# 16 bit number tables in SBUF for VectorE's one-hots, and TensorE weights read with a step, in a two-layer graph network on one Trainium2 core

## The chip, the cores and the metric

One core of one Trainium2 chip runs the whole program. The metric is device time in microseconds (us) from the first to the last instruction and what lies around it. Each engine works through its own queue of instructions and they meet by semaphores. TensorE (PE) multiplies, VectorE (DVE) and ScalarE (ACT) work element by element, GpSimd (POOL) here issues the gathers from the node tables in HBM, SyncE (SP) issues the plain transfers.

## The reference, cut to what matters

A graph with 12500 nodes of 64 features and 212500 edges, sorted by destination (`dst`). Three sums over edges are taken one after the other:

```python
msg = h[src] + edge_attr_64                        # first sum: node and edge features
agg = segment_sum(msg, dst, 12500)                 # then an MLP, batch norm, residual
out = segment_sum((x @ W)[src] * enorm, dst) + b   # second and third sum: graph convolutions
```

with layer norms, ReLUs and a graph norm around them.

## The kernel before, in words

Each of the three sums is a "pass" (k = 0, 1, 2). A pass sums most edges in one of two ways.

1. Dense windows. For each window of 125 destination nodes (54 in pass 0, 69 in passes 1 and 2) TensorE multiplies 100 blocks of edge counts (125 x 125, fp8) by the node features (125 x 192 or 193, bf16; line 1110, "app"). A window's counts are built by 25 matmuls (line 1089, "bld") of one-hots: weights `ob` of 128 edges x 125 nodes, moving operand `oh` of 128 x 300. ScalarE moves the result out as fp8 pairs (line 1211). In pass 0 all 54 windows are built and written to HBM; in pass 1 17 are built and the rest loaded; in pass 2 all are loaded.
2. Groups of 1280 edges (128 partitions x NT = 10), 167 in pass 0 and 54 in each later pass. VectorE makes a selection matrix `S` of 128 x 10 x 96 (line 971): 1 where the edge's destination less the group's first is 0 to 95. TensorE multiplies each of the ten 128 x 96 slices of it as weights by edge features (line 1125, pass 0 alone) and, for 79 of the groups of pass 0 and for all of the others, by gathered node features (line 1132). The result is folded by VectorE (line 994), turned by TensorE (line 1191) and added to the sums (line 1022).

GpSimd does the gathers: one indirect DMA for each of a group's ten columns of edges (line 1273, 128 rows of 384 bytes), with the row numbers in `srcT` in SBUF. There are 782 in pass 0 and 532 in each of passes 1 and 2. It may be NSLOT = 4 groups ahead: before the fifth it waits until TensorE is through with the first (`p_q`).

VectorE in pass 0, by the plan written out in `make_plan` (lists of steps in order of a due time, one list for each engine):

- for each bld one `oh` (line 961), a one-source operation on 300 f16 numbers with two per-partition scalars, in SBUF throughout;
- before every fifth `oh` one `ob` (line 958): is the edge's number in `modT` equal to 0..124? 5 x 125 results; the numbers 0..124 are read from PSUM in fp32 (`ps_i`), the result is f16 with the 125 nodes innermost;
- for each group one `S` (line 971), 960 results, with the numbers 0..95 read from PSUM as well; in pass 0 two subtractions of 650 fp32 numbers, both inputs in SBUF (line 987), that split the edge features into three bf16 parts;
- the folds and additions (lines 994, 1003, 1004, 1022, 1027).

Buffers: NOB = 3 tiles for `ob` (each for five bld), NOH = 6 for `oh`, NS = 2 for `S`. VectorE waits for `p_bld >= 5 (n - NOB + 1)` before the n-th `ob` and for `p_bld >= v - 5` before the v-th `oh`.

The edges' destinations reach SBUF once, at the start, as `relT` (f16), laid out column t first, group g second; the group's ten numbers lie 166 elements apart. Line 971 has ten rows of 96 results, each comparing one number of `relT` with the 96 numbers of PSUM.

## Time and profile before

| | us |
|---|---|
| median of 3 runs | 2910.58 (2907.73 to 2920.95) |
| the profiled execution | 2908.32, of which the span is 2906.8 |

Busy time of the engines over the span, from the page of the profile:

| engine | busy us | share of the span |
|---|---|---|
| PE matmuls | 2552.8 | 88% |
| PE weight loads | 2416.9 | 83% |
| DVE | 1743.1 | 60% |
| ACT | 888.7 | 31% |
| POOL | 1993.7 | 69% |

The mean granted TensorE clock was 0.956. The shares are means over stages with different limits. The gathers divide the run: pass 0 lies from 107 to 1334 us, with its gathers to 1248; then comes the batch norm, the second layer norm and a new table; the gathers of pass 1 run from 1420 to 2117, those of pass 2 from 2193 to 2856. A matmul's time is from its start to its modelled end, and matmuls overlap, so their busy time is no measure of how full TensorE is. The time of one gather instruction on POOL is the time in which GpSimd makes its descriptors; the data land some microseconds later.

### The profile page before, as it was taken

To read this page: it belongs to the slowest core of one execution; us is meant where nothing else is said; L and a number is where in the kernel's file an instruction comes from. 1 tells how busy PE (TensorE), PEld (TensorE's weight loads), DVE (VectorE), ACT (ScalarE), POOL (GpSimd) and SP (SyncE) were. 2 spreads that over 40 slices of the span, in tenths; PEclk is the share of its full clock that TensorE was granted. 3 is DMA by queue.
4 is the path that set the end of the run, shared out by engine and by line. 5 is a ranking of instruction groups with operands and counts; after the bars stand their busy time and mean duration, and the time that the engine had idled before them with its cause. 6 is when DMAs were issued, how large, how long until landed. Compare 5 with 4: busy or idle time off the path is not lost.

```text
span 2906.8 us, 64340 instructions
## 1 busy us (share of the span) xinstructions
PE 2552.8 (88%) x25984; PEld 2416.9 (83%) x25984; DVE 1743.1 (60%) x4148; ACT 888.7 (31%) x1492; POOL 1993.7 (69%) x1903
## 2 busy tenths in 40 slices
PE   0388988989888898895699999999997999999996
PEld 0277878878787787784699999999997999999996
DVE  8898999989988899895444444454430222222222
ACT  7344444444444444454522222232210000000001
POOL 6777777777777778710377777767706777777772
PEclk9899999999999999996799999999998999999998
DMA  4455565555556555543765555655557666666664
GB/s 116 118 149 144 147 171 151 155 157 153 148 160 153 150 148 168 148 125 105 231 204 201 163 200 196 211 181 179 200 186 203 221 206 214 208 213 199 199 214 131
DMA packets 341214, 503.37 MB, mean 173 GB/s; under 512 B 278659, under 2 KB 284217, under 8 KB 316082
## 3 DMA queue, kind: packets, MB, share of 16 engines
q1 hardware_dynamic: 280102, 402.60, 42.8%
q0 software_dynamic: 60192, 93.34, 14.0%
q8 instruction: 214, 3.51, 0.5%
q10 hardware_dynamic: 616, 3.20, 0.4%
q14 instruction: 90, 0.73, 0.1%
HBM read 361.86 MB, written 137.13 MB: 172 GB/s over the span
## 4 chain that ended last, share of the span: by engine, by line
PE 42%; POOL 37%; issue 11%; DVE 5%; DMA 2%; ACT 1%; SPq 1%; DVEq 0%; ACTq 0%; POOLq 0%
POOL arena L1273 37%; PE psum L1110 32%; PE psum L1089 3%; PE psum L1132 3%; PE psum L1071 1%; DMA arena<-table,srcT 1%; ACT arena L818 1%; DMA arena<-in_edge_attr_dram 1%; SPq L1288 0%; PE psum L1125 0%; PE psum L1195 0%; DMA arena<-table 0%; DVE arena L961 0%; DVE arena L834 0%; DVE arena L844 0%
## 5 line engine op out<-in xcount | busy, mean ns | idle before, releaser
L1273 POOL DMA_INDIRECT arena<-table,srcT x1840 | 1913.0, 1040 | 696.3 <-issue 626.5
L1110 PE MATMUL psum<-arena 125*125 125x193 bf16 (+1 forms) x19200 | 2009.1, 250 | 44.8 <-DMA arena<-counts 23.0
L1110 PEld LDWEIGHTS psum<-arena 125*125 125x125 fp8e4 x19200 | 1879.1, 140 | 87.1 <-DMA arena<-counts 23.5
L1211 ACT CAST arena<-psum 125x500 uint16<-125x500 f32 (+1 forms) x923 | 647.3, 711 | 1084.3 <-PE psum L1089 1079.8
L1089 PE MATMUL psum<-arena 128*125 128x300 f16 x1775 | 609.9, 346 | 31.6 <-DVE arena L961 24.5
L961 DVE TENSOR_SCALAR arena<-iota,keyT,oddT 128x300 f16<-128x300 f16 x1775 | 579.3, 353 | 1.4 <-PE psum L1089 1.3
L1089 PEld LDWEIGHTS psum<-arena 128*125 128x125 f16 x1775 | 247.8, 140 | 79.5 <-DVE arena L961 58.4
L971 DVE SCALAR_TENSOR_TENSOR arena<-relT,psum 128x960 bf16<-128x960 f16 x272 | 308.6, 1134 | 0.0
L987 DVE TENSOR_TENSOR arena<-arena 128x650 f32<-128x650 f32 (+1 forms) x334 | 272.8, 817 | 24.8 <-DMA arena<-in_edge_attr_dram 24.6
L958 DVE TENSOR_TENSOR arena<-modT,psum 128x625 f16<-128x625 f16 x355 | 281.0, 792 | 0.2 <-issue 0.2
L994 DVE TENSOR_REDUCE arena<-psum 96x65 f32<-96x195 f32 (+1 forms) x275 | 96.3, 350 | 307.4 <-PE psum L1132 303.4
L1132 PE MATMUL psum<-arena 128*96 128x192 bf16 x1846 | 201.0, 258 | 59.2 <-DMA arena<-table,srcT 59.2
L1132 PEld LDWEIGHTS psum<-arena 128*96 128x96 bf16 x1846 | 174.9, 130 | 65.6 <-DMA arena<-table,srcT 54.8
L1255 ACT ACTIVATE cneg<-cst 125x1 f32<-125x1 f32 x25 | 5.1, 203 | 685.4 <-DVE arena L1046 685.4
L1004 DVE TENSOR_REDUCE arena<-psum 125x64 f32<-125x192 f32 x192 | 67.1, 349 | 234.0 <-PE psum L1110 233.8
L1125 PE MATMUL psum<-arena 128*96 128x195 bf16 (+1 forms) x1662 | 189.5, 262 | 2.4 <-DVE arena L987 2.4
L1022 DVE SCALAR_TENSOR_TENSOR acc<-psum,acc 65x96 f32 (+1 forms) x275 | 67.3, 245 | 194.4 <-PE psum L1191 161.1
L1125 PEld LDWEIGHTS psum<-arena 128*96 128x96 bf16 (+1 forms) x1662 | 166.6, 128 | 5.2 <-issue 3.9
L1027 DVE SCALAR_TENSOR_TENSOR acc<-psum,acc 64x125 f32<-64x125 f32 x192 | 53.3, 278 | 105.5 <-PE psum L1195 96.1
L1003 DVE COPY cnt<-psum 125x1 f32<-125x1 f32 x123 | 18.7, 152 | 154.3 <-PE psum L1110 153.9
L1643 POOL TENSOR_TENSOR arena<-arena 125x1600 f32<-125x1600 f32 x3 | 8.6, 2867 | 132.9 <-DVE arena L1633 132.9
L1191 PE MATMUL psum<-ident,arena 96*65 96x96 f32 (+1 forms) x275 | 70.5, 256 | 29.5 <-DVE acc L1027 27.1
(219 smaller groups left out, 954.2 us busy)
## 6 DMA issues: line engine op xcount, KB each, us to landing
arena<-counts SPq DMA_DIRECT2D x121, 1600.0 KB
counts<-arena SPq DMA_DIRECT2D x71, 1600.0 KB, 6.1
arena<-in_edge_attr_dram SPq DMA_DIRECT2D x166, 320.0 KB
arena<-table,srcT POOLq DMA_INDIRECT x1840
table<-arena SPq DMA_DIRECT2D x8, 1050.0 KB
table<-arena SPq DMA_DIRECT2D x25, 168.0 KB
arena<-table SPq DMA_DIRECT2D x4, 1050.0 KB
arena<-in_x_dram ACTq DMA_DIRECT2D x4, 700.0 KB
```

Of the source, the lines that this page charges most:

```text
L958: dve.tensor_tensor(ob(four % NOB), mod, it, ALU.is_equal)
L961: dve.tensor_scalar(oh(v % NOH), iota1[:, :], keyT[:, v:v + 1], oddT[:, v:v + 1], ALU.is_equal, ALU.mult).then_inc(v_oh, 1)
L971: dve.scalar_tensor_tensor(out=S, in0=rel, scalar=0.0, in1=it, op0=ALU.add, op1=ALU.is_equal).then_inc(v_S, 1)
L987: dve.tensor_tensor(ebuf(e, i + 1)[0:parts, 0:nt * FE], a, upper, ALU.subtract).then_inc(v_rest1 if i == 0 else v_rest2, 1)
L994: dve.tensor_reduce(qbuf(n % 2)[:, 0:fe], ps_q.rearrange("p (s f) -> p f s", s=3)[:, 0:fe, :], X, ALU.add).then_inc(v_fq, 1)
L1089: pe.matmul(to[:, :, 2 * side:2 * side + 3], ob(v // NB4 % NOB)[:, v % NB4, :], oh(v % NOH).rearrange("p (j m) -> p j m", m=3), start=(sid ...
L1110: last = pe.matmul(ps_v[n % 2][0:PN, 0:xc], A(slot)[0:PN, j, 0:PN], Xs[0:PN, j, 0:xc], start=(j == 0), stop=(j == J - 1))
L1125: last = pe.matmul(ps_q, S[0:parts, t, :], e3(v % NEDGE)[0:parts, t, :, :], start=(t == 0), stop=(t == nt - 1 and not gathered))
L1132: last = pe.matmul(to, S[0:parts, t, :], gbuf(slot)[0:parts, t, :].rearrange("p (s f) -> p s f", s=3), start=(k > 0 and t == 0), stop=(t = ...
L1191: pe.transpose(ps_g[0:fe, 0:W], qbuf(m % 2)[:, 0:fe], ident[0:W, 0:W]).then_inc(p_win, 1)
L1211: act.copy(A2(slot)[0:PN, :, i // 2 * NWORD:i // 2 * NWORD + n_w], ps_b[at % NBANK][0:PN, :].rearrange("p (j x) -> p j x", x=NWORD)[:, :, ...
L1273: pool.indirect_dma_start(out=gbuf(slot)[0:parts, t, :], out_offset=None, in_=tables[k], in_offset=bass.IndirectOffsetOnAxis(ap=idx, axis= ...
```

## The change

- `relT` becomes [P, G, NT]: a group's ten numbers lie side by side. The host lays out the destinations accordingly; the transfer and the subtraction that fill it are of the same sizes.
- A table `nums` of 125 x 10 f16 numbers in SBUF, number d ten times in row d, is filled once in `dve_late_constants` by a copy of 1250 elements.
- `ob` (line 958) is written as 125 rows of five: `modT`'s five numbers, read 125 times, against the first five columns of `nums`. Both inputs and the output are f16, in SBUF, with step 1 innermost.
- `S` (line 971) is written as 96 rows of ten: the ten numbers of `relT`, read 96 times, against the first 96 rows of `nums`. It is a `tensor_tensor` in place of a `scalar_tensor_tensor` that added 0. Inputs f16, output bf16, all in SBUF.
- TensorE reads the weights of bld with a step of 5 elements (10 bytes) and those of the groups with a step of 10 elements (20 bytes), where it read them side by side.
- NOB goes from 3 to 2.

```diff
-NOB = 3
+NOB = 2
@@
-        relT = sb("relT", [P, NT, G], F16)
+        relT = sb("relT", [P, G, NT], F16)
+        nums = sb("nums", [P, PN, NT], F16)
+        num_dn, num_wt = nums[:, :, 0:NB4], nums[:, 0:W, :]
@@ def ob(k)
-            return part(o_ob, k, n_ob).bitcast(F16)[:, 0:NB4 * PN].rearrange("p (n d) -> p n d", d=PN)
+            return part(o_ob, k, n_ob).bitcast(F16)[:, 0:NB4 * PN].rearrange("p (d n) -> p d n", n=NB4)
@@ def sbuf(n)
+            return part(o_S, n, NT * W // 2).bitcast(BF16).rearrange("p (w t) -> p w t", t=NT)
@@ dve_late_constants
+            V(dve.tensor_copy(nums[:, :, :], iota[:, 0:PN].rearrange("p (d a) -> p d a", a=1).broadcast_to([P, PN, NT])))
@@ dve_pass, "oh"
-                        mod = modT[:, v:v + NB4].rearrange("p (n a) -> p n a", a=1).broadcast_to([P, NB4, PN])
-                        it = ps_i[:, 0:PN].rearrange("p (a d) -> p a d", a=1).broadcast_to([P, NB4, PN])
-                        dve.tensor_tensor(ob(four % NOB), mod, it, ALU.is_equal)
+                        mod = modT[:, v:v + NB4].rearrange("p (a n) -> p a n", a=1).broadcast_to([P, PN, NB4])
+                        dve.tensor_tensor(ob(four % NOB), mod, num_dn, ALU.is_equal)
@@ dve_pass, "S"
-                        rel = relT[:, :, g:g + 1].broadcast_to([P, NT, W])
-                        it = ps_i[:, 0:W].rearrange("p (a w) -> p a w", a=1).broadcast_to([P, NT, W])
-                        dve.scalar_tensor_tensor(out=S, in0=rel, scalar=0.0, in1=it, op0=ALU.add,
-                                                 op1=ALU.is_equal).then_inc(v_S, 1)
+                        rel = relT[:, g:g + 1, :].broadcast_to([P, W, NT])
+                        dve.tensor_tensor(S, rel, num_wt, ALU.is_equal).then_inc(v_S, 1)
@@ pe_pass, "bld"
-                    pe.matmul(to[:, :, 2 * side:2 * side + 3], ob(v // NB4 % NOB)[:, v % NB4, :],
+                    pe.matmul(to[:, :, 2 * side:2 * side + 3], ob(v // NB4 % NOB)[:, :, v % NB4],
@@ pe_pass, "grp", twice
-                            last = pe.matmul(ps_q, S[0:parts, t, :], e3(v % NEDGE)[0:parts, t, :, :],
+                            last = pe.matmul(ps_q, S[0:parts, :, t], e3(v % NEDGE)[0:parts, t, :, :],
```

## Rows read from the trace of the kernel before

**Rows 1.** Busy time by stage; columns: stretch and length, each engine's busy us (count), clock, DMA

```profile
106.80:1248.10 1141.30, 999.92 (x8871) 897.97 (x8872) 1030.15 (x2461) 509.18 (x791) 903.24 (x782) 0.95 0.57 152
1248.10:1334.00 85.90, 76.49 (x649) 64.93 (x646) 67.38 (x165) 33.51 (x57) 0.00 (x0) 0.92 0.52 146
1419.60:2117.40 697.80, 695.31 (x7617) 685.03 (x7616) 328.88 (x910) 198.99 (x299) 513.70 (x532) 1.00 0.58 196
2192.60:2856.40 663.80, 639.31 (x7418) 636.05 (x7419) 137.62 (x333) 17.68 (x66) 501.91 (x532) 0.98 0.64 207
```

**Rows 2.** The chain that ended last: 1100 to 1230 by line, then pieces (start, us, what)

```profile
by line: POOL arena L1273 80.3%; issue 19.9%
...
1230.01 6.22 DMA arena<-table,srcT
...
2840.56 6.49 DMA arena<-table,srcT
```

**Rows 3.** Waits of POOL and PE from 106.8 to 1248.1: total us, times, longest

```profile
POOL arena L1273 <- issue: 237.1, 778, 0.3
POOL arena L1273 <- PE psum L1125: 0.6, 2, 0.3
...
PE psum L1132 <- DMA arena<-table,srcT: 49.8, 22, 5.7
```

**Rows 4.** Groups of lines, 106.8 to 1248.1: count, busy us, mean ns, idle before

```profile
L1273 POOL DMA_INDIRECT arena<-table,srcT x780 | 900.9, 1155 | 248.8 <-issue 236.5 <-PE psum L709 11.4 <-PE psum L1125 0.6
...
L961 DVE TENSOR_SCALAR arena<-iota,keyT,oddT 128x300 f16<-128x300 f16 x1281 | 418.8, 353 | 1.4 <-PE psum L1089 1.3
L987 DVE TENSOR_TENSOR arena<-arena 128x650 f32<-128x650 f32 x310 | 254.1, 820 | 21.6 <-DMA arena<-in_edge_attr_dram 21.6
L958 DVE TENSOR_TENSOR arena<-modT,psum 128x625 f16<-128x625 f16 x257 | 203.4, 791 | 0.1
...
L971 DVE SCALAR_TENSOR_TENSOR arena<-relT,psum 128x960 bf16<-128x960 f16 x155 | 175.6, 1133 | 0.0
```

**Rows 5.** Instructions of POOL, then of DVE, in order of time (start, us) around 503

```profile
501.64 0.94 POOL L1273 DMA_INDIRECT arena<-table,srcT  x1 [0.30 <-issue]
502.88 2.23 POOL L1273 DMA_INDIRECT arena<-table,srcT  x1 [0.30 <-issue]
...
501.52 1.14 DVE L971 SCALAR_TENSOR_TENSOR arena<-relT,psum 128x960 bf16<-128x960 f16 x1
...
503.39 0.83 DVE L987 TENSOR_TENSOR arena<-arena 128x650 f32<-128x650 f32 x1
...
504.40 0.83 DVE L987 TENSOR_TENSOR arena<-arena 128x650 f32<-128x650 f32 x1
```

**Rows 6.** Groups of lines from 1419.6 to 2117.4, the gathers of pass 1

```profile
L1110 PEld LDWEIGHTS psum<-arena 125*125 125x125 fp8e4 x6269 | 593.5, 138 | 8.0
L1273 POOL DMA_INDIRECT arena<-table,srcT x530 | 511.9, 966 | 211.1 <-issue 153.9 <-DMA table<-arena 30.0 <-PE psum L1132 27.2
...
L961 DVE TENSOR_SCALAR arena<-iota,keyT,oddT 128x300 f16<-128x300 f16 x424 | 138.0, 356 | 0.0
...
L1132 PEld LDWEIGHTS psum<-arena 128*96 128x96 bf16 x500 | 44.9, 124 | 0.2
```

**Rows 7.** Groups of lines, 2192.6 to 2856.4, pass 2; PE's wait there

```profile
L1273 POOL DMA_INDIRECT arena<-table,srcT x530 | 500.1, 944 | 236.5 <-issue 236.2 <-PE psum L1132 0.3
L971 DVE SCALAR_TENSOR_TENSOR arena<-relT,psum 128x960 bf16<-128x960 f16 x53 | 60.4, 1139 | 0.0
...
PE psum L1132 <- DMA arena<-table,srcT: 9.4, 6, 3.4
```

**Rows 8.** 16 bit one-source compare of the start, groups of lines over the whole run

```profile
L602 DVE TENSOR_SCALAR arena<-arena 128x1792 bf16<-128x1792 f16 x13 | 8.4, 684 | 0.2
```

**Rows 9.** Matmuls of one group in order of time: edge features, gathered features

```profile
500.58 1.09 PE L1125 MATMUL psum<-arena 128*96 128x195 bf16 x10
...
501.50 1.01 PE L1132 MATMUL psum<-arena 128*96 128x192 bf16 x10
```

More of the change, by code:

```diff
@@ L13 @@
 U16 = mybir.dt.uint16
-U8 = mybir.dt.uint8
 X = mybir.AxisListType.X
@@ L346, in sbuf, with sbuf_rows @@
         def sbuf(n):
+            return part(o_S, n, NT * W // 2).bitcast(BF16).rearrange("p (w t) -> p w t", t=NT)
+        def sbuf_rows(n):
             return part(o_S, n, NT * W // 2).bitcast(BF16).rearrange("p (t w) -> p t w", w=W)
@@ L728, in dve_lists @@
             dve.wait_ge(l_dst, 2 * 16)
-            firsts = base_b[:, 0:G].rearrange("p (a g) -> p a g", a=1).broadcast_to([P, NT, G])
-            dve.tensor_tensor(relT[:, :, :], dst_i.rearrange("p (t g) -> p t g", g=G), firsts, ALU.subtract).then_inc(
+            firsts = base_b[:, 0:G].rearrange("p (g a) -> p g a", a=1).broadcast_to([P, G, NT])
+            dve.tensor_tensor(relT[:, :, :], dst_i.rearrange("p (g t) -> p g t", t=NT), firsts, ALU.subtract).then_inc(
                 v_list, 1)
@@ L738, in dve_check_lists @@
         def dve_check_lists():
-            every = relT.rearrange("p t g -> p (t g)")
+            every = relT.rearrange("p g t -> p (g t)")
             dve.wait_ge(v_list, 2)
@@ L968, in dve_pass @@
                     if g < G:
-                        rel = relT[:, :, g:g + 1].broadcast_to([P, NT, W])
-                        it = ps_i[:, 0:W].rearrange("p (a w) -> p a w", a=1).broadcast_to([P, NT, W])
-                        dve.scalar_tensor_tensor(out=S, in0=rel, scalar=0.0, in1=it, op0=ALU.add,
-                                                 op1=ALU.is_equal).then_inc(v_S, 1)
-                    else:
-                        rel = relh_l[0:R, :].rearrange("p (t a) -> p t a", a=1).broadcast_to([R, 2, W])
-                        it = ps_i[0:R, 0:W].rearrange("p (a w) -> p a w", a=1).broadcast_to([R, 2, W])
-                        dve.scalar_tensor_tensor(out=S[0:R, 0:2, :], in0=rel, scalar=0.0, in1=it, op0=ALU.add,
-                                                 op1=ALU.is_equal).then_inc(v_S, 1)
+                        rel = relT[:, g:g + 1, :].broadcast_to([P, W, NT])
+                        dve.tensor_tensor(S, rel, num_wt, ALU.is_equal).then_inc(v_S, 1)
+                    else:
+                        rel = relh_l[0:R, :].rearrange("p (a t) -> p a t", a=1).broadcast_to([R, W, 2])
+                        dve.tensor_tensor(S[0:R, :, 0:2], rel, num_wt[0:R, :, 0:2], ALU.is_equal).then_inc(v_S, 1)
                 elif kind in ("rest1", "rest2"):
@@ L1131, in pe_pass @@
                         for t in range(nt):
-                            last = pe.matmul(to, S[0:parts, t, :],
+                            last = pe.matmul(to, S[0:parts, :, t],
                                              gbuf(slot)[0:parts, t, :].rearrange("p (s f) -> p s f", s=3),
@@ L1420, in slow_group @@
             pool.sem_clear(t_idx)
-            gb, S = gbuf(0), sbuf(0)
+            gb, S = gbuf(0), sbuf_rows(0)
             for t in range(nt):
@@ L1982 @@
     laid['x'] = x.reshape(-1, PN, F).transpose(1, 0, 2).reshape(PN, -1)
-    for name, a in (('src_turned', src), ('dst_turned', dst)):
-        laid[name] = a[0:n_groups * P * NT].reshape(n_groups, P, NT).transpose(1, 2, 0)
+    for name, a, order in (('src_turned', src, (1, 2, 0)), ('dst_turned', dst, (1, 0, 2))):
+        laid[name] = a[0:n_groups * P * NT].reshape(n_groups, P, NT).transpose(*order)
     behind = _np.stack([_np.full(P, n_nodes, dst.dtype), _np.zeros(P, dst.dtype)], axis=1)
```

2 lines of the change are left out of this document (1 added, 1 removed).

## The prediction

> **What bounds the kernel now.** I read first the busy times by stage [rows 1]: in pass 0 (106.8 to 1248.1 us) DVE is busy 1030.2 of 1141.3 us, so at first sight VectorE is the bound and a cut of its work should pay. Then I read the chain of work that ended last [rows 2]: from 1100 to 1230 us it consists of the gathers' instructions on POOL (80.3%) and of "issue" (19.9%), and nothing else. The waits say the same [rows 3]: over all of pass 0 POOL waited for a free slot, which PE releases, hardly at all (0.6 us in the row of L1125), only 0.3 us between one gather and the next (778 times, 237.1 us), while PE waited 49.8 us for gathered data. POOL never stops, and it is never ahead by its four groups. So POOL sets pass 0, and until its end: the gather that lands at 1236 us, the piece of 6.22 us [rows 2], is the last on the chain. The full VectorE is a coincidence there.
>
> What does a gather cost? 1155 ns on the mean in pass 0, 966 in pass 1, 944 in pass 2 [rows 4, 6, 7]. Pass 2 has no `oh` and no edge splitting, and 944 is the undisturbed price. Pass 0 pays 0.211 us more, 782 times: 165 us. The order of time around 503 us shows when [rows 5]. The gather at 501.64 took 0.94 us although line 971 ran on VectorE from 501.52 to 502.66: that instruction reads one input in SBUF and one in PSUM. The gather at 502.88 took 2.23 us, and the two splits of line 987 at 503.39 and 504.40, both inputs in SBUF, lie inside it. In pass 2 line 971 runs beside the gathers 53 times and they still average 944 ns [rows 7]. So GpSimd is held up by VectorE when the latter takes two numbers at a time from SBUF (line 987, and line 961, the 16 bit operation of one source), not when one input comes from PSUM.
>
> In pass 1 PE is busy 695.3 of 697.8 us and POOL has slack: 27.2 us of waits for PE's slots [rows 1, 6]. In pass 2 PE and POOL are level: POOL goes without a pause, and PE, busy 639.3 of 663.8 us, waits 9.4 us for gathers; the last gather is on the chain at 2840.6 us [rows 1, 2, 7].
>
> **The change part by part.**
>
> VectorE's own time. Lines 958 and 971 (625 and 960 results, 791 and 1133 ns, rows 4) give (1133 - 791)/335 = 1.02 ns a result and 154 ns that are fixed. After the change all operands have 16 bits, lie in SBUF and run side by side. No two-source operation of that kind is in the trace. Its bounds are 1.02 ns (nothing gained) and the one-source operation of line 602, (684 - 154)/1792 = 0.30 ns [rows 8]. That one reads one number for each result; with the same reading a two-source one would need 0.6. I take half of 1.02, the nearest to that: 473 and 644 ns. In pass 0 the 257 + 155 instructions then need 122 + 100 = 222 us in place of 379: 157 us less. The Trainium skill, "VectorE: DVE Perf Modes", section "The perf-mode tier table", also gives a two-source 16 bit operation two results a cycle at best; no run shows it yet. By the rows above this saving lies beside POOL's chain and is worth nothing before 1248 us. In the last stage of pass 0 (to 1334 us, no gathers, DVE busy 67.4 of 85.9 us, rows 1) 13 of pass 0's 270 `ob` and 12 of its 167 `S` are left: 13 x 0.32 + 12 x 0.49 = 10 us less, of which I count half, -5 us.
>
> What VectorE now takes from POOL. Both lines turn from one SBUF input into two. This is the dear part. I measure the disturbance by the share of a stage in which VectorE runs such instructions. Pass 0: (418.8 + 254.1)/1141.3 = 59% and 0.211 us a gather; pass 1: 138.0/697.8 = 20% and 0.022 us [rows 4, 6]. The disturbance grows by 9.6 where the share grows by 3.0, so about with its square (instructions that follow each other directly hold GpSimd up through all of them, as the 2.23 us show). After the change, pass 0 has 672.9 + 222 = 895 us of it in some 1227 us, 73%: 0.211 x (0.73/0.59)^2 = 0.323 us, 0.11 more for each of 782 gathers, +86 us. Bounds: with the share itself, not its square, +40 us; with no wait at all for 16 bit inputs, 0; if VectorE does not become faster (1.02 ns), 1052 us of it, +150 us. POOL's later gathers queue behind the one held up, PE waits for them at line 1132, and all of PE's later windows stand behind that. As POOL has no slack in pass 0, all of the +86 us reach the end.
> Pass 1: 138.0 + 85 x 0.473 + 53 x 0.644 = 212 us, 30%: 0.030 us more for 530 gathers, 16 us, hidden in the 27.2 us that POOL waits there. That cover would be gone if the rise were twice as large. Pass 2: 53 `S` alone. A gather comes every 1.25 us (944 ns and 0.3); it falls into an `S` of 0.644 us every second time and waits 0.32 us: 53 x 0.5 x 0.32 = 8.5 us at most; by the square rule under 1 us. I take +4 us, on the path.
> The Trainium skill, "SBUF — State Buffer", section "Who interferes with whom", has the rule that speaks against this change: a VectorE instruction with two SBUF inputs contends with a GpSimd instruction that reads SBUF. By that rule 16 bits make no difference; the trace agrees for fp32 inputs alone.
>
> The table: one copy of 1250 numbers, by line 971's price 1250 x 1.02 + 154 = 1.4 us, in the start where VectorE is on the path: +1.4 us. Between 0 (hidden behind row sums) and 1.4.
>
> NOB = 2: the n-th `ob` (v = 5n) waits for v - 5 bld, the same number for which the `oh` right behind it waits already. VectorE waited 1.4 us in all at line 961 [rows 4]. 0 us.
>
> Weights with a step. Loads of 125 and 96 columns took 138 and 124 ns [rows 6], so 0.48 ns a column: 60 and 46 ns of streaming, under matmuls that follow each other every (1.01 - 0.25)/9 = 84 ns [rows 9]. Nothing in the trace loads 16 bit weights with a step. The nearest is the moving operand of line 1125, every second 16 bit number: ten take 1.09 us, against 1.01 us [rows 9], 8 ns each with three columns more. Gain is excluded, since the columns stay. A load twice as long comes out at 92 ns for the groups and 120 for bld, against the 84: it nearly hides; at three times it does not. I take 0, the nearest row being close to 0; twice is 500 x 0.008 + 424 x 0.036 + 530 x 0.008 = 23 us (passes 1 and 2; in pass 0 PE has room).
>
> Laying out `relT` the other way: same transfer and same 1660 results, 0.
>
> Sum: +86 - 5 + 1.4 + 0 + 4 = +86 us on the profiled execution's 2908.3 us: 2995 us. That execution lies 2.3 us under the median of the three runs, so I forecast **2997 us** for the median. From the bounds of the disturbance alone its range is 2950 to 3060.
>
> **The rivals.**
>
> *16 bit inputs don't hold GpSimd up* (other side). For: all rows of a two-source instruction that delays are fp32. Against: line 961 is 16 bit throughout, and the gathers of pass 1 that it lengthens have hardly another cause. Then pass 0 keeps POOL's 1141 us: -5 + 1.4, 2907 us. If in addition VectorE's idle time (busy share from 90% to 76%) breaks up the rows of instructions that hold POOL, the 165 us of disturbance could shrink by a fifth, -35 us: 2872 us. It decides where the mean gather of pass 0 stays below 1155 ns. 18%.
>
> *The stepped weights cost three times the streaming time.* The groups' matmuls then come every 138 ns (+54) and those behind a bld load 96 ns later: (155 + 78) x 10 x 0.054 + 1281 x 0.096 = 249 us in pass 0, PE's 1000 us become 1249, 22 more than POOL's 1227; pass 1, where PE has no idle time, 500 x 0.054 + 424 x 0.096 = 68 us; pass 2 530 x 0.054 = 28 us. With the 86 and the offset of the median: 2997 + 22 + 68 + 28 = 3115 us. It decides above twice. For: nothing measured; against: the row of line 1125. 12%. The Trainium skill, "Advanced Engine Details and Errata", section "Memory Cachelines", says that SBUF wants two hits on a line of 16 bytes for full speed; a step of 20 bytes never gives two. Its price for a miss is not stated, and no row here shows one.
>
> *The comparison does not go side by side* (rows of 5 or 10, re-read inputs, five being odd). Lines 958 and 971 stay at 0.8 and 1.1 us but with two SBUF inputs: +150 us in pass 0, 4 over the cover in pass 1, 12 in pass 2: 3077 us. 6%.
>
> **How the numbers follow.** Forecast 62%, the rivals 18%, 12% and 6%, 2% for something else. A measurement of this kernel can tell about 0.5%, 14.6 us, from no change. The forecast holds over 2925 us but for 3 in 100 (VectorE's gaps undo the contention). Of the first rival's 18% I put half on each side of 2896 us. Faster 0.09, same 0.15 (9 and 3 of these, and 3 of a mix), slower 0.76. The range must reach to the first rival's upper half and the third rival, and to mild costs of the step: 2890 to 3100 us.
>
> **What would show it.** Lines 958 and 971 at 473 and 644 ns (right) or at 0.8 and 1.1 us (third rival). The mean gather in pass 0 at 1.27 us (right), at or under 1.155 (first rival); over 944 ns in pass 2 by up to 16 ns. VectorE's busy time in pass 0 down by 157 us and pass 0 longer all the same, with PE's wait for gathers above 49.8 us. Ten matmuls of a group still in 1.0 to 1.1 us, the 96 column load near 124 ns (right) or far over it (second rival). The forecast is wrong if POOL is no longer on the chain in pass 0.

## The result and the profile after

| | median of the runs | profiled execution |
|---|---|---|
| before | 2914.8 us (4 runs, 2907.7 to 2921.0) | 2908.3 us, span 2906.8 |
| after | 3107.9 us (4 runs, 3104.9 to 3109.4) | 3108.4 us, span 3106.9 |

The changed kernel takes 1.0662 times as long (95% interval 1.0632 to 1.0692), 193 us more. The forecast was 2997 us, its range ended at 3100. The sign was right, the size (86 us) less than half, and the busy times by stage show where.

The busy times by stage of the changed kernel (columns as in rows 1, one stretch more at the end, from the last gather of pass 2 to the end of the span):

```profile
108.40:1344.00 1235.60, 1187.70 (x8824) 1108.66 (x8825) 899.91 (x2451) 508.74 (x787) 997.45 (x782) 0.98 0.52 140
1344.00:1440.00 96.00, 92.75 (x695) 81.18 (x693) 63.70 (x175) 36.60 (x62) 0.00 (x0) 0.96 0.49 140
1525.40:2284.90 759.50, 757.59 (x7612) 747.77 (x7611) 284.72 (x910) 199.12 (x298) 543.72 (x532) 1.00 0.55 181
2362.30:3036.40 674.10, 656.48 (x7206) 654.20 (x7207) 108.03 (x322) 16.88 (x63) 512.05 (x532) 0.99 0.63 201
3036.40:3106.90 70.50, 48.60 (x531) 47.53 (x528) 17.35 (x45) 10.35 (x18) 0.00 (x0) 0.84 0.43 121
```

Against [rows 1]: pass 0 is 94 us longer, the stage behind its last gather 10, pass 1 62, pass 2 10, and the end behind its last gather (50.4 us before, from 2856.4 to the span's end) 20. With 4 us at the start and between the passes that is the whole 200 us between the two profiled spans. VectorE's busy time in pass 0 fell from 1030 to 900 us. TensorE's rose from 1000 to 1188 in pass 0, from 695 to 758 in pass 1 and from 639 to 656 in pass 2: with the same instructions at another step. The granted clock is the full one or nearly so in the three passes, and nowhere there lower than before, so the clock is no part of it.

Groups of lines of the changed kernel: pass 0 (108.4 to 1344.0), then its two comparisons over the whole run, then pass 1 (1525.4 to 2284.9), then pass 2 (2362.3 to 3036.4):

```profile
L1273 POOL DMA_INDIRECT arena<-table,srcT x780 | 995.5, 1276 | 248.9 <-issue 236.3 <-PE psum L714 11.4 <-PE psum L1132 0.9
L1089 PEld LDWEIGHTS psum<-arena 128*125 128x125 f16 x1271 | 280.8, 222 | 44.9 <-DVE arena L965 27.6 <-issue 16.4
L1125 PEld LDWEIGHTS psum<-arena 128*96 128x96 bf16 x1540 | 271.2, 261 | 0.8 <-issue 0.7
...
L962 DVE TENSOR_TENSOR arena<-modT,nums 128x625 f16<-128x625 f16 x355 | 191.8, 540 | 6.2 <-PE psum L1089 5.9
L974 DVE TENSOR_TENSOR arena<-relT,nums 128x960 bf16<-128x960 f16 x272 | 174.6, 642 | 0.0
...
L1273 POOL DMA_INDIRECT arena<-table,srcT x530 | 541.9, 1023 | 242.0 <-issue 150.9 <-PE psum L1132 60.9 <-DMA table<-arena 30.2
L1132 PEld LDWEIGHTS psum<-arena 128*96 128x96 bf16 x500 | 87.4, 260 | 0.0
...
L1273 POOL DMA_INDIRECT arena<-table,srcT x530 | 510.3, 963 | 238.8 <-issue 238.8
```

Two things happened at once. A gather takes 1276 ns in pass 0 where it took 1155 [rows 4]. And a weight load of 96 columns takes 260 ns where it took 124 [rows 6]; that of bld (125 columns) 222, about 140 before. The order of time around 503 us, TensorE's matmuls, shows what the load costs (columns as in rows 9; the first three rows are consecutive bld):

```profile
502.20 0.39 PE L1089 MATMUL psum<-arena 128*125 128x300 f16 x1
502.77 0.39 PE L1089 MATMUL psum<-arena 128*125 128x300 f16 x1
503.34 0.39 PE L1089 MATMUL psum<-arena 128*125 128x300 f16 x1
...
499.40 1.83 PE L1132 MATMUL psum<-arena 128*96 128x192 bf16 x10
...
505.69 1.84 PE L1125 MATMUL psum<-arena 128*96 128x195 bf16 x10
```

Ten matmuls of a group took 1.09 and 1.01 us [rows 9] and take 1.84 and 1.83. By the median of all starts they follow each other every 167 ns, where it was 92 (line 1125) and 85 (line 1132). A bld with its four window matmuls comes every 0.57 us where it was 0.51.

The chain of work that ended last, by line, in pass 0 and in pass 1:

```profile
by line: POOL arena L1273 41.2%; PE psum L1110 12.2%; issue 10.1%; PE psum L1125 8.7%; PE psum L1089 8.7%; DMA arena<-in_edge_attr_dram 6.4%; PE psum L1132 4.6%; DVE arena L987 1.7%; DMA arena<-table,srcT 1.0%; PE psum L1145 1.0%; PE psum L
...
by line: PE psum L1110 69.5%; PE psum L1089 12.5%; PE psum L1132 10.9%; PE psum L1071 2.5%; PE psum L1176 1.2%; PE psum L1195 1.0%; PE psum L1157 0.8%; PE psum L1191 0.5%; DVEq L1020 0.5%; issue 0.3%; DVE acc L1022 0.2%; DVE arena L1004 0.0
```

Pass 0 was POOL's alone [rows 2]; now TensorE and POOL share it. Pass 1 is TensorE's alone. The waits of pass 0 (columns as in rows 3) say the same:

```profile
POOL arena L1273 <- issue: 236.9, 777, 0.3
...
POOL arena L1273 <- PE psum L1132: 0.9, 3, 0.3
...
PE psum L1132 <- DMA arena<-table,srcT: 24.2, 8, 6.3
```

POOL still goes without a pause, but TensorE waits for its gathers 24.2 us where it waited 49.8 [rows 3]: both are full.

### The profile page after: what moved, and what is told of

Same layout as the page of the kernel before. It is cut to its first block, busy times and chain, and to the rows that moved or that the text cites. A ratio compares the mean times of both kernels' runs of the same rounds, so it can differ in the third digit from the quotient of the medians.

```text
span 3106.9 us, 64341 instructions
## 1 busy us (share of the span) xinstructions
PE 2858.6 (92%) x25984; PEld 2747.8 (88%) x25984; DVE 1539.0 (50%) x4149; ACT 891.7 (29%) x1492; POOL 2125.9 (68%) x1903
## 4 chain that ended last, share of the span: by engine, by line
PE 66%; POOL 16%; DVE 5%; issue 5%; DMA 4%; ACT 1%; SPq 1%; DVEq 1%; ACTq 0%; POOLq 0%
PE psum L1110 43%; POOL arena L1273 16%; PE psum L1132 8%; PE psum L1089 7%; PE psum L1125 4%; DMA arena<-in_edge_attr_dram 3%; PE psum L1071 1%; DVE arena L987 1%; PE psum L1195 1%; PE psum L1191 1%; PE psum L1148 1%; PE psum L1145 1%; ACT arena L823 1%; DMA arena<-table 0%; DVEq L1020 0%
## 5 line engine op out<-in xcount | busy, mean ns | idle before, releaser
L1273 POOL DMA_INDIRECT arena<-table,srcT x1840 | 2047.7, 1113 | 729.7 <-issue 626.0
L1089 PE MATMUL psum<-arena 128*125 128x300 f16 x1775 | 696.3, 395 | 11.1 <-DVE arena L965 5.9
L1089 PEld LDWEIGHTS psum<-arena 128*125 128x125 f16 x1775 | 391.5, 221 | 48.2 <-DVE arena L965 29.9
L1132 PE MATMUL psum<-arena 128*96 128x192 bf16 x1846 | 338.6, 333 | 24.2 <-DMA arena<-table,srcT 24.2
L1132 PEld LDWEIGHTS psum<-arena 128*96 128x96 bf16 x1846 | 323.8, 260 | 26.2 <-DMA arena<-table,srcT 25.9
L1125 PE MATMUL psum<-arena 128*96 128x195 bf16 (+1 forms) x1662 | 305.2, 331 | 0.3 <-DVE arena L987 0.3
L1125 PEld LDWEIGHTS psum<-arena 128*96 128x96 bf16 (+1 forms) x1662 | 292.7, 261 | 1.4 <-issue 1.2
L962 DVE TENSOR_TENSOR arena<-modT,nums 128x625 f16<-128x625 f16 x355 | 191.8, 540 | 6.2 <-PE psum L1089 5.9
L974 DVE TENSOR_TENSOR arena<-relT,nums 128x960 bf16<-128x960 f16 x272 | 174.6, 642 | 0.0
```

The lines of the kernel that those rows point to most:

```text
L962: dve.tensor_tensor(ob(four % NOB), mod, num_dn, ALU.is_equal)
L974: dve.tensor_tensor(S, rel, num_wt, ALU.is_equal).then_inc(v_S, 1)
L1089: pe.matmul(to[:, :, 2 * side:2 * side + 3], ob(v // NB4 % NOB)[:, :, v % NB4], oh(v % NOH).rearrange("p (j m) -> p j m", m=3), start=(sid ...
L1125: last = pe.matmul(ps_q, S[0:parts, :, t], e3(v % NEDGE)[0:parts, t, :, :], start=(t == 0), stop=(t == nt - 1 and not gathered))
L1132: last = pe.matmul(to, S[0:parts, :, t], gbuf(slot)[0:parts, t, :].rearrange("p (s f) -> p s f", s=3), start=(k > 0 and t == 0), stop=(t = ...
L1273: pool.indirect_dma_start(out=gbuf(slot)[0:parts, t, :], out_offset=None, in_=tables[k], in_offset=bass.IndirectOffsetOnAxis(ap=idx, axis= ...
```

## The experiments

The expectations name three theories, formed on the two traces. Theory A: there are two causes, the second SBUF input of the comparisons, which holds GpSimd up (the forecast's mechanism), and the steps of 10 and 20 bytes, which cost TensorE (the forecast's second rival). Theory B: the steps alone cost time, and the longer gathers nothing. Theory C: the longer gathers alone.

The experiments do one part alone, put the step at other sizes, and put the numbers at other places. Each kernel is an edit of the changed one, so all of them have NOB = 2 and the new layout of `relT`; the cuts of code below are against the changed kernel (that of e12 against e9). Each is measured against the kernel before, on the same chip. "Stretch" is from the first gather of a pass to the end of its last. "One result a cycle" stands for 1.02 ns a result, the price of lines 958 and 971 before; "two a cycle" for half of that.

| kernel | weights' step, bytes | numbers of the comparisons | time, us | ratio to before (95%) | mean gather, passes 0 / 1 / 2, ns | stretches, us |
|---|---|---|---|---|---|---|
| before | 2 | fp32, PSUM | 2915 to 2919 | | 1155 / 966 / 944 | 1141 / 698 / 664 |
| after | 10, 20 | 16 bit, SBUF | 3107.9 | 1.0662 (1.0632 to 1.0692) | 1276 / 1022 / 963 | 1236 / 759 / 674 |
| e1 | 10, 20 | fp32, PSUM | 3098.5 | 1.0627 (1.0595 to 1.0659) | 1124 / 964 / 946 | 1190 / 761 / 665 |
| e2 | S alone, 20 | fp32, PSUM | 3036.2 | 1.0417 (1.0384 to 1.0449) | 1144 / 964 / 944 | 1156 / 739 / 664 |
| e3 | ob alone, 10 | fp32, PSUM | 2933.9 | 1.0060 (1.0027 to 1.0093) | 1152 / 963 / 944 | 1139 / 720 / 664 |
| e10 | S alone, 10 | fp32, PSUM | 2927.1 | 1.0035 (1.0020 to 1.0051) | 1145 / 963 / 944 | 1134 / 712 / 664 |
| e4 | 2 | 16 bit, both inputs SBUF | 2990.2 | 1.0262 (1.0226 to 1.0298) | 1250 / 1008 / 960 | 1215 / 698 / 672 |
| e5 | 2 | 16 bit, SBUF, one result a cycle | 3197.0 | 1.0971 (1.0938 to 1.1004) | 1466 / 1066 / 1001 | 1385 / 729 / 694 |
| e11 | 10, 20 | 16 bit, PSUM | 3090.2 | 1.0598 (1.0573 to 1.0623) | 1095 / 963 / 944 | 1185 / 760 / 664 |
| e6 | S alone, 4 | S: 16 bit pairs, PSUM | 2905.4 | 0.9965 (0.9951 to 0.9978) | 1148 / 963 / 943 | 1136 / 697 / 664 |
| e7 | S alone, 4 | S: pairs, SBUF | 3039.7 | 1.0423 (1.0394 to 1.0451) | 1293 / 1001 / 985 | 1249 / 698 / 686 |
| e8 | as e6 | as e6, and those of oh in PSUM | 2899.0 | 0.9931 (0.9909 to 0.9954) | 1086 / 946 / 943 | 1095 / 697 / 664 |
| e9 | S and ob, 4 | all in PSUM, pairs | 2874.3 | 0.9868 (0.9829 to 0.9907) | 1067 / 946 / 943 | 1073 / 697 / 664 |
| e12 | as e9 | as e9, even start | 2858.2 | 0.9805 (0.9787 to 0.9823) | 1061 / 947 / 945 | 1068 / 697 / 664 |

Before has steps of 2 bytes, that is, weights side by side.

**e1: the steps alone.** The changed kernel's layouts, with the numbers read where they were (PSUM, fp32, one result a cycle):

```diff
-                        dve.tensor_tensor(S, rel, num_wt, ALU.is_equal).then_inc(v_S, 1)
+                        it = ps_i[:, 0:W].rearrange("p (w a) -> p w a", a=1).broadcast_to([P, W, NT])
+                        dve.tensor_tensor(S, rel, it, ALU.is_equal).then_inc(v_S, 1)
```

(`ob` likewise.)

> The kernel after, but VectorE's numbers come from PSUM in fp32 as before (one SBUF input for each compare, one result a cycle). TensorE still reads the weights with steps of 10 and 20 bytes. Theory A (two causes: the stepped weights cost TensorE, and the second SBUF input costs GpSimd): the gather of pass 0 goes back to about 1155 ns, passes 1 and 2 stay as long as in the kernel after (762 and 674 us for their gathers), the 96 column load stays at 260 ns; VectorE's compares at 0.79 and 1.14 us. Pass 0 is then set by TensorE or VectorE alone: 3020 to 3090 us in all. Theory B (the steps alone are the cause, the longer gathers cost nothing): 3108 us, as after. Theory C (the gathers alone): 2915 us, as before.

Groups of lines over the whole run:

```profile
L1275 POOL DMA_INDIRECT arena<-table,srcT x1840 | 1888.5, 1026 | 832.4 <-issue 613.6 <-PE psum L1134 177.0 <-DMA table<-arena 30.4
...
L1091 PEld LDWEIGHTS psum<-arena 128*125 128x125 f16 x1775 | 391.1, 221 | 51.2 <-DVE arena L966 34.4 <-issue 16.3
L1134 PEld LDWEIGHTS psum<-arena 128*96 128x96 bf16 x1840 | 322.7, 260 | 9.1 <-DMA arena<-table,srcT 9.1
```

The steps alone cost 182 of the 193 us. That is 8 us over theory A's range and 9 us under theory B's 3108. No gather is slower than before (1124 ns in pass 0); POOL now waits 177 us for TensorE's slots. Pass 1 is as long as after the whole change (761 against 759 us). In pass 0 TensorE was busy 1148 of 1190 us, and from the last gather of pass 0 to the first of pass 1 it took 216 us where it took 171 before: TensorE is behind, and catches up there. The same shows at the end: the stretch of pass 2 is as before, but behind its last gather 79 us pass until the end of the span, where it was 50.

**e2 and e3: each step alone.** `S` as rows of ten with dense `ob`, and the reverse.

> Only the groups' weights (S) are read with a step (20 bytes); the numbers come from PSUM, the one-hots ob are as before. In the kernel after ten matmuls of a group take (1.84 - 0.33)/9 = 168 ns each in place of 84 to 92. If that is TensorE's price for this step: pass 1 500 x 0.083 = +41 us, pass 2 at most 530 x 0.083 = +44 us less what POOL sets there anyway (30 in the kernel after), pass 0 2330 x 0.083 = 193 us of TensorE time, 1193 against POOL's 1141: +50 us. About 3035 us. If the time of the step-only kernel came from ob: 2960 us.

> Only the one-hots' weights (ob) are read with a step (10 bytes); numbers from PSUM, S laid out and read as before. A bld with its four window matmuls took 0.567 us in the kernel after and 0.513 before: +54 ns. Pass 1 424 x 0.054 = +23 us, pass 2 nothing, pass 0 69 us of TensorE time that lie beside POOL's chain: 0 to +15 us. About 2945 us.

These two, e8 and e9 first ran on a chip on which the kernel before took 4254 us, at a granted clock of 0.83; TensorE's loads of line 1110 (1113 in e3) there stood 457 us at "issue" in e3, against 11.6 us on another chip. The ratios from that chip (1.034 for e2, 1.011 for e3, 1.042 for e8, 1.043 for e9) say nothing of a stage, and all four were run again elsewhere; the table has those.

> The kernel that steps only in S once more, because the kernel before took 4254 us in that comparison and TensorE was held up from outside. On a chip where before takes about 2915 us: loads of 96 columns at 260 ns, pass 1 +41 us, pass 2 up to +44 us, pass 0 set by TensorE: 3035 us. If ob is the greater part of the steps' price: 2960 us.

> The kernel that steps only in ob, once more for the same reason: loads of 125 columns at 221 ns, +54 ns for each bld, pass 1 +23 us, pass 0 up to +15 us: 2945 us.

`S` alone costs 117 us, as expected (3035 us expected, 3036 measured); `ob` alone 15 (2945 expected, 2934 measured). In pass 1, where TensorE is the bound, they add up: 41 and 23 us of stretch, 63 in e1. In pass 0 they don't: `S` alone 55 us (14 in the stretch and 40 behind it), `ob` alone nothing (the stretch is 2 us shorter), both together 93. Before the change TensorE had 141 us of idle time there [rows 1], which takes up the first part of whatever it has to do more.

**e10: S with half the step.** `S` as two blocks of 96 rows of five, so 10 bytes from column to column; `ob` dense.

```diff
-                            last = pe.matmul(to, S[0:parts, :, t],
+                            last = pe.matmul(to, S[0:parts, t // 5, :, t % 5],
```

> S in two blocks of 96 x 5, so its weights are read with a step of 10 bytes in place of 20; numbers from PSUM in fp32, ob as before. If the price is per column and grows with the step (1.14 ns a column at 10 bytes, as ob's loads show, 1.9 ns at 20): loads of 187 ns, ten matmuls 25 ns apart more than before, pass 1 +12 us, pass 2 +13 us, pass 0 hidden: 2940 us. If any step beyond a few bytes costs the same: 260 ns and 3036 us as with 20 bytes.

Groups of lines over the whole run, and ten matmuls in the order of time:

```profile
L1134 PEld LDWEIGHTS psum<-arena 128*96 128x96 bf16 x1840 | 227.9, 208 | 33.2 <-DMA arena<-table,srcT 33.2
...
503.94 1.27 PE L1127 MATMUL psum<-arena 128*96 128x195 bf16 x10
```

The matmuls follow each other every 113 ns: 1.18 ns a column at 10 bytes against 167/96 = 1.74 ns at 20. The kernel loses 11.4 us where it lost 117 (2940 us expected, 2927 measured). Of the longer beat, 14 us show in the stretch of pass 1 and none in that of pass 2, where TensorE had idle time [rows 1].

**e6: S in pairs, numbers in PSUM.** Five blocks of 96 pairs, 4 bytes from column to column; the numbers as 16 bit, each twice, in PSUM.

```diff
-                        rel = relT[:, g:g + 1, :].broadcast_to([P, W, NT])
-                        dve.tensor_tensor(S, rel, num_wt, ALU.is_equal).then_inc(v_S, 1)
+                        rel = relT[:, g, :].rearrange("p (h a t) -> p h a t", a=1, t=2).broadcast_to([P, NT // 2, W, 2])
+                        it = ps_p.rearrange("p (a w) t -> p a w t", a=1).broadcast_to([P, NT // 2, W, 2])
+                        dve.tensor_tensor(S, rel, it, ALU.is_equal).then_inc(v_S, 1)
```

> Both causes taken away while the compare of the groups keeps running side by side: S is laid out as five blocks of 96 pairs, so the weights are read with a step of 2 elements (4 bytes), and the 16 bit numbers, each twice, lie in PSUM, so only one input comes from SBUF. The one-hots ob are as before (numbers from PSUM, weights side by side). Theory A: if a step of 4 bytes hides under the matmul, loads near 130 to 150 ns and ten matmuls in 1.0 to 1.1 us; gathers at 1155 ns or a little less; 2880 to 2920 us. If any step costs: 3000 us or more. If 16 bit numbers in PSUM don't run side by side, the compare stays at 1.13 us and the time at 2915 us.

Groups of lines over the whole run:

```profile
L1138 PEld LDWEIGHTS psum<-arena 128*96 128x96 bf16 x1840 | 173.9, 130 | 88.3 <-DMA arena<-table,srcT 78.6 <-issue 9.5
...
L980 DVE TENSOR_TENSOR arena<-relT,psum 128x960 bf16<-128x960 f16 x272 | 173.0, 636 | 0.0
```

A step of 4 bytes is free: 130 ns a load, and the beats of 92 and 85 ns of the kernel before. And the comparison runs two a cycle with an input in PSUM (636 ns against 1133), while the gathers stay at 1148 ns. This is the change's aim for `S` without its two costs, and it buys 11 us (0.9965, interval 0.9951 to 0.9978): the saving of VectorE in pass 0 is worth little, as the forecast had it (it put 155 x 0.5 us beside POOL's chain).

**e4: two SBUF inputs alone.** Dense weights; both comparisons read rows of 16 bit numbers from SBUF on both sides and run side by side. The numbers compared are others, so `ob` and `S` aren't the right ones; sizes and types are.

```diff
-                        rel = relT[:, g:g + 1, :].broadcast_to([P, W, NT])
-                        dve.tensor_tensor(S, rel, num_wt, ALU.is_equal).then_inc(v_S, 1)
+                        rel = iota1[:, g:g + W].rearrange("p (a w) -> p a w", a=1).broadcast_to([P, NT, W]) if g + W <= KC else \
+                            iota1[:, 0:W].rearrange("p (a w) -> p a w", a=1).broadcast_to([P, NT, W])
+                        it = line16[:, 0:W].rearrange("p (a w) -> p a w", a=1).broadcast_to([P, NT, W])
+                        dve.tensor_tensor(S, rel, it, ALU.is_equal).then_inc(v_S, 1)
```

(`ob` likewise; TensorE reads both with no step.)

> Weights lie side by side as before; both compares read two 16 bit rows in SBUF with step 1 and run two results a cycle. To have step 1 in this layout they compare other 16 bit numbers of SBUF, so selection matrices and one-hots are not those of the reference, and the answer of the check of the counts is left out so that the slow path isn't taken. Theory A: loads at 130 and 140 ns as before; the compares at 473 to 540 and 644 ns; the gather of pass 0 at 1265 ns, so pass 0 86 us longer, pass 1 hidden, pass 2 4 us: 3000 us. Theory B: 2915 us or less. Theory C (the gathers alone explain the whole loss): 3108 us.

Groups of lines over the whole run, then the chain of pass 0 (110 to 1320 us) by line:

```profile
L1279 POOL DMA_INDIRECT arena<-table,srcT x1840 | 2018.5, 1097 | 675.0 <-issue 632.3 <-DMA table<-arena 30.0 <-PE psum L716 11.4
L979 DVE TENSOR_TENSOR arena<-iota,line 128x960 bf16<-128x960 f16 x272 | 175.8, 646 | 0.0
L965 DVE TENSOR_TENSOR arena<-iota,line 128x625 f16<-128x625 f16 x355 | 169.3, 477 | 4.5 <-PE psum L1095 3.5
...
by line: POOL arena L1279 78.6%; issue 19.1%; DMA arena<-table,srcT 0.9%; PE psum L1116 0.7%; PE psum L1095 0.3%; PE psum L1138 0.3%; PE psum L1131 0.2%; PE psum L1197 0.0%; PE psum L1201 0.0%
```

This is the forecast's kernel, and it behaves as forecast: 74 us in the median (stretch of pass 0 +74, pass 1 0, pass 2 +9), the gather at 1250 ns, POOL's chain alone, 477 and 646 ns. So 16 bit inputs in SBUF do hold GpSimd up, and theory C's 3108 us is out as well: both causes are there.

**e5: the same at one result a cycle.** The layout of before, `S` read across rows, the numbers in 16 bit from SBUF.

> The layout of before, weights side by side, right numbers, but the 16 bit numbers 0..127 come from SBUF in place of PSUM: two SBUF inputs, one result a cycle (the other input repeats one number). One cause alone, and longer than in the kernel after. Theory A: compares at 0.79 and 1.13 us; by the square of the share of time the gather of pass 0 at 1.35 us, +150 us in pass 0: 3065 to 3080 us. Theory B: 2915 us. If the gather waits depend on the operation's rate and not on its time, the same 3000 us as the fast compares.

798 and 1139 ns a comparison, a mean gather of 1466 ns in pass 0 and 280 us in all, 117 us above the top of the expected range. The square rule expected some 0.40 us over 944 ns, the trace shows 0.52: the rule doesn't hold here. The other branch, the same 3000 us as with fast comparisons, is out as well: the kernel is 207 us slower than e4. e5 also measures the forecast's third rival, which had 150 us for it in pass 0; the stretch rose by 243.

**e11: the steps with side by side comparisons, numbers in PSUM.** The changed kernel without its second SBUF input.

```diff
-                        dve.tensor_tensor(S, rel, num_wt, ALU.is_equal).then_inc(v_S, 1)
...
+                        it = num_dn[:, 0:W, 0:2].rearrange("p w (a t) -> p w a t", a=1).broadcast_to([P, W, NT // 2, 2])
```

> The kernel after with its steps of 10 and 20 bytes and VectorE's compares side by side, but the 16 bit numbers lie in PSUM: the second SBUF input alone is taken away. If in pass 0 TensorE with stepped weights is the bound by itself, the gathers fall back to 1150 ns and the time to that of the slow compares with stepped weights, 3098 us, or up to 10 us under it: contention then costs only 10 to 20 us on top of the steps. If POOL was the bound in the kernel after, pass 0 falls by up to 94 us: 3015 us.

3090 us, as expected for a pass 0 set by TensorE. Against the changed kernel 18 us are left for the contention, which alone (e4) is worth 74. Pass 0, with what lies behind it up to pass 1, is 87 us longer than before here and 104 after the whole change.

**e7: e6 with the numbers in SBUF.** The pairs are taken from `nums`, so they lie 20 bytes apart.

> S in pairs (weights with a step of 4 bytes), its numbers in SBUF as in the kernel after, ob as before from PSUM. Steps cost nothing there; only the 272 S take two SBUF inputs. By the square of the share, (672.9 + 100)/1165 = 66% against 59%: +0.056 us for each of 782 gathers, +44 us, and +4 us in pass 2: 2960 us. If S alone doesn't hold GpSimd up (ob did): 2905 us, as with the numbers in PSUM.

Group of lines over the whole run:

```profile
L977 DVE TENSOR_TENSOR arena<-relT,nums 128x960 bf16<-128x960 f16 x272 | 272.1, 1001 | 0.0
```

Missed by 80 us. The expectation took 644 ns for the comparison; pairs 20 bytes apart take 1001, so VectorE holds GpSimd longer (1293 ns a gather). The share of pass 0 in which VectorE runs instructions of the disturbing kind is only 66% here ((672.9 + 155 x 1.0)/1249) against 74% in e4, and the gathers are longer than there. So the share isn't the right measure.

**When a gather waits.** Pass 2 shows it, because there the comparisons of `S` are the only ones of this kind beside the gathers. Two places of e5's trace, gathers first, then comparisons:

```profile
2489.30 0.94 POOL L1278 DMA_INDIRECT arena<-table,srcT  x1 [0.30 <-issue]
2498.19 1.71 POOL L1278 DMA_INDIRECT arena<-table,srcT  x1 [0.30 <-issue]
...
2489.67 1.15 DVE L978 TENSOR_TENSOR arena<-relT,line 128x960 bf16<-128x960 f16 x1
2497.94 1.14 DVE L978 TENSOR_TENSOR arena<-relT,line 128x960 bf16<-128x960 f16 x1
```

The first comparison began 0.37 us after the start of its gather, and the gather took its 0.94 us all the same. The second ran when its gather began and had 0.89 us to go: the gather took 0.77 us more. The whole of pass 2 in the changed kernel, e4, e5 and e7 goes like this. A gather that begins during such a comparison is longer by what is left of it, less some 0.12 us (0.10 to 0.17 where more than 0.15 us are left). One in which the comparison begins more than 0.16 us after its start is longer by 13 ns at most (118 gathers). One in which it begins before that waits for all of it or not at all. With the numbers in PSUM (e6) the 66 gathers that touch a comparison take 943 ns, as the others. So a gather waits once, close to its start, for the end of the comparison, and the price goes with the square of the length of one instruction: an estimate from a gather every 1.25 us and 53 comparisons of length L is 53 x L x L/2.5, which gives 9, 22 and 28 us for 0.65, 1.01 and 1.14 us; pass 2 became 9 (e4), 22 (e7) and 30 us (e5) longer. In pass 0 disturbing instructions of three kinds follow each other, so that the same isn't shown for each of them there.

**e8, e9 and e12: the numbers of `oh` and `ob` in PSUM as well.** e8 is e6, and line 961's 300 numbers lie in PSUM as well. e9 adds `ob` in pairs (three blocks of 125 pairs, so six numbers of `modT` instead of five). e12 starts the six numbers at an even place of `modT`:

```diff
-                        mod = modT[:, v:v + 6].rearrange("p (h a t) -> p h a t", a=1, t=2).broadcast_to([P, 3, PN, 2])
+                        mod = modT[:, v - v % 2:v - v % 2 + 6].rearrange("p (h a t) -> p h a t", a=1, t=2).broadcast_to([P, 3, PN, 2])
```

> On top of the pairs kernel (16 bit numbers for S in PSUM) the 300 numbers of the one-hots oh are read from PSUM in 16 bits as well, so that VectorE's 1775 oh no longer take both SBUF ports; only the splits of the edge features still do. If GpSimd is held up by whatever uses VectorE's second port in SBUF: by the square of the share of time, (254/1100)^2 against (673/1141)^2, the gather of pass 0 falls from 1148 ns to about 980 ns; a count of the gathers that touch splits gives 1050 ns. POOL's stretch falls by 75 to 130 us and VectorE (974 us busy, plus 0.05 us for each of 1281 oh) or TensorE (992 us) becomes the bound of pass 0: 2840 to 2880 us. If oh matters little beside the splits: 2900 us.

> On top of the former, the one-hots ob are made in pairs too (three pairs of 125 numbers, the sixth left over, 750 results, 16 bit numbers in PSUM, weights with a step of 4 bytes). An ob should fall from 0.79 to 0.154 + 750 x 0.51 = 0.54 us: 270 x 0.25 = 67 us less on VectorE in pass 0. If VectorE became the bound of pass 0 in the former kernel, up to 50 us less than there; if POOL or TensorE still set it, the same time as there within 10 us.

> The kernel that reads the numbers of oh from PSUM in 16 bits, once more for the same reason. There the mean gather of pass 0 was 1017 ns and an oh took 423 ns in place of 353. POOL alone would then need 782 x (1.017 + 0.303) = 1032 us for pass 0; VectorE needs 974 + 1281 x 0.07 = 1064 us. Pass 0's gathers in 1070 to 1130 us in place of 1136: 2840 to 2900 us, set by VectorE.

> The kernel that has ob in pairs as well, once more for the same reason. There an ob took 728 ns, not the 540 expected, so VectorE gains only 270 x 0.065 = 18 us on the former kernel: the same time as that within 15 us.

> The kernel with all numbers in PSUM, but an ob whose five numbers begin at an odd place reads six numbers from the even place before it. If the odd start keeps the pairs from going side by side, every ob takes 528 ns (now 528 and 917 in turn): VectorE 135 x 0.39 = 53 us less in pass 0. If POOL alone sets pass 0, its length hardly moves (1072 us, less what shorter VectorE work gives the gathers, 0 to 20 us): 2855 to 2875 us in all. If VectorE still set it, 2835 us. If the odd start isn't the cause, 722 ns on the mean and 2874 us.

`ob` in the order of time in e9 (two instructions that follow each other on this line), then its group and that of line 970 (`oh`) in e12:

```profile
501.15 0.54 DVE L967 TENSOR_TENSOR arena<-modT,psum 128x750 f16<-128x750 f16 x1
506.08 0.93 DVE L967 TENSOR_TENSOR arena<-modT,psum 128x750 f16<-128x750 f16 x1
...
L970 DVE TENSOR_SCALAR arena<-psum,keyT,oddT 128x300 f16<-128x300 f16 x1775 | 700.1, 421 | 0.9 <-PE psum L1095 0.9
L967 DVE TENSOR_TENSOR arena<-modT,psum 128x750 f16<-128x750 f16 x355 | 188.5, 531 | 0.4
```

`oh` from PSUM takes 63 ns more of VectorE (419 for 356) and 62 ns less of each gather of pass 0 (1148 to 1086), and the stretch of pass 0 shrinks by 40 us. In the profiled executions all of that comes back behind its last gather (212 us up to pass 1 in place of 172); the medians of e6 and e8, measured in two comparisons, are 6 us apart. The chain says why. In e6 74.8% of it in pass 0 is POOL's; in e8, from 110 to 1204 us, it is:

```profile
by line: DVE arena L971 14.4%; PE psum L1117 12.1%; DMA arena<-in_edge_attr_dram 10.8%; DVE arena L994 8.8%; PE psum L1096 7.2%; PE psum L1132 7.1%; issue 7.0%; POOL arena L1280 6.8%; DVE arena L968 4.7%; PE psum L1139 4.2%; DVEq L1027 2.4%
```

So with the gathers undisturbed by `oh`, POOL no longer sets pass 0: VectorE, TensorE and the loads of edge features do, in turn. e8 came at the upper end of what was expected (2840 to 2900 us, set by VectorE). e9 is 25 us faster than e8, where 15 at most were expected: VectorE's time now counts. With the even start every `ob` takes 531 ns instead of 0.53 and 0.92 in turn. That is 37 us less of VectorE in the stretch of pass 0 (992 to 955 us), and the kernel is 16 us faster for it. e12 is 2% faster than the kernel before, and the fastest of all. POOL goes without a pause in its stretch of pass 0 (782 x (1.061 + 0.303) = 1067 of 1068 us), but it is 22.8% of the chain there, and 194 us pass up to pass 1 where it was 171: the other engines end the pass.

## Why the prediction was right or wrong

- *POOL sets pass 0 and a faster VectorE is worth nothing there.* Right. VectorE was busy 130 us less in pass 0 (157 forecast) and the stage longer all the same, and e6, which takes half a microsecond from each `S` and disturbs no one, shortened the stretch of pass 0 by 5.5 us. It holds only while the gathers are disturbed: from e8 to e12 VectorE's time was worth something.
- *473 and 644 ns.* `S` 642: right, so two results a cycle. `ob` 540, 67 ns over. e4's `ob`, with rows of 125, takes 477; the changed one has rows of five, as e11's (535 ns with a dense table in PSUM), so it is the short rows. Why five cost and ten don't stays open.
- *The second SBUF input holds GpSimd up, +86 us in pass 0, hidden in pass 1, +4 in pass 2.* The mechanism and the size were right: 1.27 us forecast, 1250 ns in e4 and 1276 after; +74, 0 and +9 us in e4. The first rival fell with it. But the square of VectorE's share, from which the 86 us came, isn't the rule: a gather waits for the end of one instruction, so the length of the instructions decides, and e5 and e7 came 117 and 80 us over what the share gave. That it came so near for the change itself is partly luck. In pass 2 the count of the forecast (8.5 us at most) was the right one, not the 4 us taken from it. In pass 1 a gather grew by 42 ns in e4 where 30 were forecast, and was hidden all the same. One reading was a little off: the second of the two splits around 503 us [rows 5] ends at 505.23, 0.12 us after the gather of 2.23 us; it lies not quite inside it.
- *Weights with a step: 0.* This is the step of the forecast that failed: a cost put at nothing from a row that didn't bear on it. The nearest row was a moving operand with every second 16 bit number, a step of 4 bytes, and e6 shows that 4 bytes are free for weights as well. The change has 10 and 20. I treated a row at another step as near because it was the only one, and reached for twice the streaming as the worst. Measured: 85 ns of beat at 2 and 4 bytes, 113 at 10, 167 at 20, so 1.74 ns a column where 0.48 was taken, 3.6 times. The term of 0 (23 at twice) should have been 182 alone (e1), in pass 0 as well, where the forecast gave TensorE room.
- *The second rival.* Its sum, 3115 us, was 7 us off, and its terms by stage are those of the trace: pass 1 +68 (62 measured), pass 2 +28 (30 with the end behind its last gather), pass 0 just above POOL's time. It had the step for bld at +96 ns a load (54 measured) and for the groups at +54 ns a matmul (75 and 82 measured). That the sum came out is luck: in pass 0 the two errors cancel (1281 x 0.054 + 1550 x 0.075 + 780 x 0.082 = 249 us, as forecast), and in pass 2 a beat 82 ns longer would be 43 us, of which 30 reach the end. It had a chance of 12%, and the range stopped 15 us short of it. A cost that the trace bounds from neither side, and that falls on an engine busy 695 of 698 us [rows 1], deserved a range that reaches to it. The rule that the prediction cited beside it, of the Trainium skill, "Advanced Engine Details and Errata", section "Memory Cachelines" (two hits on a line of 16 bytes), agrees with the three steps in its order: eight columns of a line at 2 bytes and four at 4 are free, one or two at 10 cost, one at 20 costs most. The lines themselves no run shows.
- *The two costs together.* Steps alone 182, contention alone 74, both 193. In pass 0 POOL and TensorE go side by side: the steps raise TensorE to 1188 us of 1236, the gathers raise POOL to 782 x (1.276 + 0.303) = 1235 us, and the stage takes about the longer one, not the sum: up to the first gather of pass 1, the steps alone cost 93 us (e1), the contention alone 70 (e4), both 104. That was in the rival's arithmetic (1249 against 1227) and held.
- *Wrong if POOL is no longer on the chain in pass 0.* It is, with 41% of the chain of pass 0 (73.7% before, over 110 to 1248 us; the 80% of rows 2 are those of 1100 to 1230 us): a test of this kind has to name the engine that joins. *TensorE's wait for gathers above 49.8 us.* It fell to 24.2, the first sign in the waits that TensorE had become slower.
- *NOB = 2, the table, the other layout of `relT`: 0, 1.4, 0 us.* The first gather begins 1.6 us later (108.4 against 106.8). VectorE waits 6.2 us in all at line 962 in the whole run. e6 has all three too and is 11 us faster than the kernel before, so they can't cost much.

## What to carry to other kernels

A layout that serves the engine that writes has a price at the one that reads: before an operand of TensorE gets a step, look at whether TensorE has slack in every stage, keep the step of weights at 4 bytes, and take pairs (4 bytes) where a whole row isn't needed for two results a cycle. A faster VectorE is worth something only where it is on the chain. Where GpSimd's gathers are on it, put one of VectorE's inputs in PSUM, or make its instructions shorter, and look at which engine sets the stage then: e8 took 40 us off POOL's stretch and gave them back behind it. Where a term has no near row, price the rival on the engine that has no idle time first.

## What the runs showed of the hardware

- Weight loads with a step, 16 bit: at 4 bytes as side by side (130 ns for 96 columns, beat 92 and 85 ns); at 10 bytes 208 ns, beat 113; at 20 bytes 260 ns, beat 167. 125 columns at 10 bytes: 221 ns against 140.
- A comparison of 16 bit numbers with one input in PSUM runs two results a cycle (960 in 636 ns) and leaves GpSimd alone: gathers of 943 ns in pass 2 of e6, with 53 of them beside.
- A comparison with both inputs in SBUF holds up a gather that begins while it runs until it ends, and leaves a gather alone that began more than 0.16 us before it (pass 2 of the changed kernel, e4, e5, e7).
- VectorE has its own price for places of numbers: rows of two that start at an odd 16 bit number of `modT` take 0.92 us in place of 0.53 (e9, 750 results, the other input in PSUM); pairs 20 bytes apart in SBUF 1001 ns in place of some 640 (e7, 960 results), pairs 10 bytes apart in PSUM 885 (e11). For the first, the Trainium skill, "Vector Engine (DVE) Microarchitecture Reference", section "5.1 Performance modes — why throughput varies by op and dtype", says that 4 byte alignment makes no difference with two sources; e9 and e12, alike but for the start, show the opposite for rows of two, and the measurement decides. (`modT` itself is taken to start at a multiple of 4 bytes.) `ob` in rows of five starts at odd places half the time too, and takes 540 ns throughout.
- The 300 numbers of `oh`: 354 ns from SBUF, 421 from PSUM (e12).
- The mean gather of pass 0 with VectorE beside it: 1061 ns (e12), 1155 (before), 1250 (e4), 1276 (after), 1466 (e5); 944 undisturbed. All three kinds of instruction are in it: fp32 with two sources, 16 bit with two (e4), and 16 bit with one (`oh`: e6 to e8, 1148 to 1086 ns).
